# A fused transformer kernel on one core: the hand-kept order of five engines' work, set anew for all 16 groups

## The reference

```python
# layer 0
x = x + tanh(g_xattn[0]) * xattn(layernorm(x), ctx)     # 8 heads, 128 keys, rope, softmax, Wout
h = bitlinear(layernorm(x), w_fc) + gate * low_rank     # 512 -> 2048, ternary weights
x = x + tanh(g_ffn[0]) * bitlinear(relu(h) ** 2, w_proj)
# layer 1
x = x + tanh(g_xattn[1]) * (layernorm(x) @ W1.T + mean(ctx) @ W2.T + b)
h = act_quant(rmsnorm(layernorm(x))) @ ternary(w1).T + b1   # 512 -> 2048
x = x + tanh(g_ffn[1]) * (act_quant(rmsnorm(gelu(h))) @ ternary(w2).T + b2)
```

## Time and profile before

| what | value |
|---|---|
| median of 3 runs | 1218.28 us (1217.88 to 1218.72) |
| the profiled execution's own time | 1217.09 us |
| its span in the trace | 1215.3 us |
| PE busy in the span | 1099.9 us (91%) |
| DVE, ACT, POOL busy | 959.9, 795.2, 590.3 us |
| mean granted clock of PE | 0.977 of full speed |

### The profile page before, as it was taken

One profiled execution on the slowest core, in us unless ns is written; L12 is line 12 of the kernel. 1 busy time (PEld: TensorE's weight loads), 2 busy tenths in 40 slices (PEclk: granted clock), 3 DMA queues, 4 the chain that ended last, 5 costly groups with the idle time before them and its releaser, 6 DMA issues.

```text
span 1215.3 us, 22111 instructions
## 1 busy us (share of the span) xinstructions
PE 1099.9 (91%) x8254; PEld 681.4 (56%) x8542; DVE 959.9 (79%) x1993; ACT 795.2 (65%) x1557; POOL 590.3 (49%) x569
## 2 busy tenths in 40 slices
PE   5766888999999998999999989999999999999995
PEld 5544646565656555564657565654756566564642
DVE  4696689887889797888978897888869677877766
ACT  3887847666675848485756749484675929494624
POOL 2442556454546455464645465554546364563440
PEclk9878999999999999999999999999999999999997
DMA  9959472433427362435434452624345261433132
GB/s 322 361 157 280 148 195 47 95 82 81 105 48 140 57 133 55 104 80 100 88 66 105 66 128 51 126 60 102 71 79 122 48 139 34 102 70 78 23 61 65
DMA packets 281225, 129.93 MB, mean 107 GB/s; under 512 B 254992, under 2 KB 255504, under 8 KB 279440
## 3 DMA queue, kind: packets, MB, share of 16 engines
q1 hardware_dynamic: 280560, 127.57, 45.6%
q10 hardware_dynamic: 560, 0.96, 0.3%
HBM read 57.19 MB, written 8.39 MB: 54 GB/s over the span
## 4 chain that ended last, share of the span: by engine, by line
PE 42%; ACT 23%; DVE 22%; DMA 6%; issue 4%; POOL 3%; SPq 0%; ACTq 0%; DVEq 0%
PE ps L1780 12%; ACT e L949 5%; PE ps L1731 5%; PE ps L1814 4%; PE ps L1682 4%; PE ps L1830 4%; ACT rl L981 4%; PE ps L1764 4%; ACT hid L986 3%; ACT sq L992 2%; DVE st L1342 2%; DVE amax L1075 2%; PE ps L1797 2%; ACT p L957 1%; DMA pt<-p 1%
## 5 line engine op out<-in xcount | busy, mean ns | idle before, releaser
L1764 PE MATMUL ps<-xT,fcT 128*128 128x256 f16 x2048 | 258.7, 274 | 10.0 <-ACT rl L981 9.9
L738 POOL TENSOR_TENSOR rs<-ve,nhalf 128x1 f32<-128x1 f32 x160 | 103.8, 651 | 327.5 <-DVE ve L1347 231.0
L1780 PE MATMUL ps<-pjT,hid 128*128 128x512 fp8e4 x1024 | 232.7, 379 | 5.0 <-issue 2.7
L1764 PEld LDWEIGHTS ps<-xT,fcT 128*128 128x128 fp8e4 x2048 | 199.4, 98 | 49.0 <-ACT rl L981 13.7
L763 POOL TENSOR_TENSOR hid<-sq,hid 128x512 f16<-128x512 f32 x128 | 156.5, 1226 | 104.0 <-ACT sq L992 103.3
L1780 PEld LDWEIGHTS ps<-pjT,hid 128*128 128x128 f16 x1024 | 97.7, 98 | 98.1
L1814 PE MATMUL ps<-w1T,q4T 128*128 128x512 fp8e4 x480 | 118.5, 380 | 9.1 <-DVE h L1491 5.0
L981 ACT ACTIVATE rl<-ps,rsf 128x256 f32<-128x256 f32 x256 | 106.4, 468 | 29.7 <-PE ps L1768 29.5
L949 ACT ACTIVATE e<-ps,nmb,sig 128x128 f32<-128x128 f32 x256 | 113.1, 459 | 16.8 <-DVE nmb L1385 16.7
L1830 PE MATMUL ps<-w2T,hT 128*128 128x512 fp8e4 x480 | 108.4, 379 | 7.3 <-DMA hT<-q 7.3
L1491 DVE SCALAR_TENSOR_TENSOR h<-ps,dqs,b1bc 128x512 f32<-128x512 f32 x120 | 87.9, 743 | 25.8 <-PE ps L1814 24.8
(11 more groups left out here) (234 smaller groups left out, 2032.8 us busy)
## 6 DMA issues: line engine op xcount, KB each, us to landing
...
h<-in_wkvT SPq DMA_DIRECT2D x2, 1024.0 KB, 12.8
hid<-in_w_fc SPq DMA_DIRECT2D x2, 1024.0 KB, 10.9
```

Source lines behind the costliest of these rows:

```text
L738: pool.tensor_tensor(rs[:, n, t:t + 1], ve[:, n, t:t + 1], nhalf[:, :], ALU.pow).then_inc(done, 1)
L1764: pe.matmul(dst, fcT[:, k, f * P:(f + 1) * P], xT2[:, xs, k, :], start=(xs == 0 and k == 0), stop=False)
L1780: mm = pe.matmul(ps[:, FFN0 + t, :], hid[:, xs, c, t * P:(t + 1) * P], pjT[:, c, :], start=(c == 0 and xs == 0), stop=(c == FC - 1 and xs ...
```

## The change

All place numbers of `ORDER` and `PREP` are set anew; nothing else is touched. Each engine holds the same pieces as before. Only a few lines of the table are shown here, since its numbers say little by themselves:

```diff
         ORDER = dict(
             PE=dict(
-                up=((32, 33, 34, 36, 37, 38, 39, 40), (59, 60, 61, 62, 63, 65, 70, 72),
+                up=((33, 34, 35, 36, 37, 38, 39, 40), (59, 60, 61, 62, 63, 65, 69, 70),
...
-                s=((13,), (35,), (58,), (94,), (132,), (167,), (201,), (237,), (273,), (312,), (344,), (384,),
+                s=((13,), (32,), (57,), (96,), (133,), (168,), (200,), (237,), (273,), (308,), (349,), (382,),
```

More of the change, by code:

```diff
@@ new lines, in build @@
+                x1_hi=((0, 2), (8, 31), (48, 75), (107, 112), (135, 146), (165, 174), (200, 202), (231, 235),
+                       (257, 266), (286, 296), (323, 328), (354, 359), (382, 393), (411, 419), (454, 455),
+                       (481, 482)),
+                rot=((17, 18), (51, 52), (85, 86), (116, 118), (151, 152), (178, 181), (209, 210), (240, 242),
+                     (270, 273), (301, 302), (333, 337), (363, 365), (396, 398), (425, 427), (460, 462),
+                     (486, 487)),
@@ L542, in build @@
-            ACT=dict(wq=(3,), k_hi=(17,), v_hi=(20, 22), tanh=(0,), wo=(15,), evac=(6, 13, 16, 23, 28, 36, 37, 38),
-                     rows=(4, 7, 11, 19), whole=(5, 8, 14, 21), low=(32,), wx=(42,),
-                     sums=(27, 33, 40, 43, 44, 45, 46, 47), lift=(52, 55, 58, 74, 75, 79, 81, 85)),
-            POOL=dict(whole=(14, 19, 20, 21), rot_k=(4, 5), csb=(6,), low_zero=(13,)),
-            SP=dict(u=(1,), rows=(6,), ctx=(0,), wk=(3,), wq=(2,), wv=(7,),
-                    piece=(4, 8, 14, 20, 19, 16, 22, 24, 25, 27, 31, 34, 35, 26, 30, 38, 39, 40, 45, 46, 48, 53, 54, 58),
-                    wo=(15,), wc=(11,), wx=(5,), b1=(18,)))
+            PE=dict(k=(2, 3), v=(5, 6), low=(0,), mix=(15,), tern=(4, 7, 12, 14, 16, 19, 20, 21), low_t=(17,),
+                    row_scale=(24,), mean=(30,), spread=(1, 8, 9, 18, 23)),
@@ new lines, in build @@
+            ACT=dict(wq=(4,), k_hi=(15,), v_hi=(14, 20), tanh=(1,), wo=(12,), evac=(6, 10, 16, 22, 27, 36, 37, 38),
+                     rows=(3, 7, 11, 19), whole=(5, 9, 13, 21), low=(32,), wx=(42,),
+                     sums=(26, 33, 40, 43, 44, 45, 49, 50), lift=(54, 59, 66, 72, 74, 77, 79, 80)),
+            POOL=dict(whole=(13, 19, 20, 21), rot_k=(5, 6), csb=(4,), low_zero=(12,)),
+            SP=dict(u=(0,), rows=(13,), ctx=(3,), wk=(4,), wq=(1,), wv=(7,),
+                    piece=(2, 10, 14, 20, 19, 18, 21, 23, 24, 26, 31, 34, 35, 25, 30, 38, 39, 43, 45, 47, 49, 52, 53, 57),
+                    wo=(6,), wc=(5,), wx=(11,), b1=(17,)))
```

249 lines of the change are left out of this document (121 added, 128 removed), and 126 rows, old and new, of tables (down, exp, h, hid).

## The result

| | before | changed |
|---|---|---|
| median | 1218.08 us (1217.59 to 1218.72, 4 runs) | 1207.78 us (1205.83 to 1209.11, 4 runs) |
| ratio to before | | 0.9914, interval 0.9896 to 0.9931 |
| the profiled execution's own time, its span | 1217.09, 1215.3 us | 1205.83, 1204.0 us |

In what follows "waits of PE" are the idle times in the brackets of PE's timeline rows, added up from `low` of group 0 (its own wait not counted) to the last `w2` 0: 70.0 us before, 66.8 after.

The account below looks back on a forecast made before the run. The prediction took PE, busy 1099.9 of 1215.3 us, to bound the kernel, so only its waits could change. Its terms summed to -0.1 us, 1217.0 against the profiled execution's 1217.09, hence a median of 1218.2; range 1208 to 1228.

Parts of the forecast that it names:

- The quantity: Whole kernel: judge an order by cover, the PE work between a piece and the one needing it, against the engines between.
- The start, -1.5: Up to the first values product: scores start some 2 us earlier, the later chain gives part back; -1.5 us.
- Group 0 with group 1, +0.1: 120 to 187 us: waits at scores, `q` and `wx` go, but ACT's later last `up` costs +5.4; together +0.1 us.
- `low` and `up` 0: Groups 1, 10, 13: `up` 0 directly behind `low` waits 1.46 each for the low-rank part; old waits partly go; +2.4 us.
- `w2` 0 of group 2: Cover behind `w1` 3 falls from 19.2 to 14.6 us; PE waits between nothing and 3.1; +1.6 us taken.
- `q`: `q` behind `wo`: more cover in groups 5, 10, 13 gives -2.3, less in group 9 costs +1.0; sum -1.3 us.
- `wx` 1 of group 14: Cover behind `down` 7 falls from 12.8 to 7.4 us; wait 1.6 to 3.5; +2.6 us taken.
- `wx` behind the output write: Three places gain cover, 4.0 us of waits go; group 9 loses its cover, costing 1.2; sum -2.8 us.
- `w2` behind `w1`: `w2` 1 behind `w1` 7: waits in groups 9 and 6 go, group 8 gets +2.0; sum -1.2 us.
- The faster one: Rival for the whole kernel: relu waits, 8.1 us, go and the two middle-group losses stay away; -8.4, 1210 us; chance 0.33.
- The slower rival: `up` rows wait for ACT, with a gap of over 4 us in group 0; +8.8, 1225 to 1227 us; chance 0.31.
- The second price: Group 0's `up` row: after a long gap PE's clock drops to half, adding up to 2.7 us; within the slower rival.

Follow-up runs that it names:

- n2_order: Against the kernel before: all five engines in a new order that counts SP's queue times, with spare in every cover; 1196.58 us, ratio 0.9805.
- n1_order: Against the kernel before: all five engines in a third order, set by covers and DVE's holds by POOL; ratio 1.0189, slower by 23 us.
- x3_pe: The kernel before with PE's order alone made anew; ratio 1.0003 to before, +0.4 us.
- e2_rest: The kernel before up to group 2's scores, the changed kernel's order from there, on all engines; ratio 0.9931 to before, -8.4 us.
- e3_tail: The kernel before up to group 15's scores, the changed kernel's order from there, on all engines; ratio 0.9983 to before, -2.1 us.
- e6_mid: The kernel before with the changed kernel's order only from group 2's to group 15's scores; ratio 0.9982 to before, -2.2 us.
- e1_start: The kernel before with the changed kernel's order only up to `low` of group 0, on all engines; ratio 0.9973 to before, -3.3 us.
- d1_dve: The changed kernel with two 32-column pad writes per layer-norm statistic on DVE instead of one of 1 column; ratio 0.9943 to before.
- n4_both: The changed kernel's order up to `low` of group 0, then that of n3_order, on every engine; ratio 0.9789 to before.
- n5_both: Like n4_both, but the order behind `low` of group 0 set anew for the earlier start; ratio 0.9774 to before.
- e5_relu: The kernel before with six `up` on ACT moved ahead of the exponentials or gelu they stood behind; ratio 1.0059, slower by 7.2 us.
- n3_order: Against the kernel before: all five engines ordered by the rules of n2_order from another start; 1192.73 us, ratio 0.9783.

## Why the prediction was wrong, step by step

*The quantity.* PE's work is the same in all 18 kernels, and its waits go with their times: 49.5 to 52.4 us of waits with medians of 1192 to 1197 us, 62 to 73 with 1208 to 1220, 75.5 with 1226 and 85 with 1243. Inside the second band they don't rank the kernels. Nor are the waits the whole price: PE's busy time for the same matmuls was 1092.9 us in n2_order and 1109.9 in n1_order, at mean granted clocks of 0.976 and 0.962. What failed is that the waits can be read from covers on PE. The mean covers that I compared speak of PE's order alone, and in x3_pe another order of PE alone moved nothing.

*The start, -1.5.* The step that failed is that `low`'s own wait of 5.12 us was left out of the sum. It fell to 1.35. Not even that is its whole size: `mean` came 4.0 us earlier in the changed profile, but in e2_rest, e3_tail and e6_mid, with the start of before, it came at 111.7 to 112.0 us too, and `low` then waited 7.2 to 7.4; in the four other kernels with the new start (e1_start, d1_dve, n4_both, n5_both) it waited 1.3 to 3.0. So the new start is worth 5 us or so there. The scores of group 0 came 4.4 us earlier than in the profile of before, 2.5 earlier than in e6_mid's, where some 2 were expected. But the larger lead was worth little in the end: 3.3 us alone (e1_start), nothing measurable in n4_both.

*Group 0 with group 1, +0.1.* The 0.9 for the scores of group 1 went as forecast. On ACT the size was about right and the place was not: relu and `down` together cost PE 6.3 us more (4.4 to 10.7) where 5.4 stood in the sum, but as a wait of 7.45 in the middle of the `up` row, not as lateness at its end. Wrong were the waits said to go, -4.0: `q` of group 2 waits 3.12 for DVE and `wx` 0 1.49, together 4.6 instead of the two waits' 4.0 of before. From `low` of group 0 to group 2's scores, these included, PE's waits rose by 4.8 instead of 0.1.

*From group 2's scores on, +1.3 for six terms and 0 for the tail.* `low` and `up` 0: +2.5 at L1768, forecast 2.4. `w2` 0 of group 2: 1.89, forecast 1.6. `q`: -0.9, forecast -1.3. These were good. `wx` 1 of group 14: 1.21, forecast 2.6. `wx` behind the output write: -1.4, forecast -2.8. `w2` behind `w1`: all waits for hT fell by 2.8 (with the 1.9 of group 2 in them), so about -4.6 for the rest against -1.2. The step that failed beside this last one is that two lists were put at nothing, without a reason: relu waits at L1764, 8.1 to 1.0, and `w1`'s for L1491, 5.0 to 2.0, while others that were not in the sum (scores, probabilities, `w1` for its transposes) rose by some 4. In all, these waits went from 59.9 to 51.5 us, -8.4 instead of +1.3: -3.4 up to group 15's scores, -5.0 from there. The term for the tail itself, behind the last `down` of group 15, held: 13.8 to 14.6. What went lies just ahead of it, 1.6 at `low` of group 15, 1.1 at its scores, 1.3 for hT and 1.0, 0.8, 0.6 and 0.6 at `w1` and `up`, and no term stood for it. The forecast's own sign of being wrong, idle time that moves by more than 7 us there, came; that of the start, more than 5, did not.

*The rivals.* The faster one named relu and 1210, and the time was 1207.8. Its condition was met in part: relu's waits fell by 7.2, but the two losses that it left out came, at 1.9 and 1.2. That relu's waits are what was won isn't shown: thinning them from ACT's side made the kernel slower (e5_relu). That they fell because DVE and ACT as a whole were set anew is likely, not shown. The slower rival's gap in group 0 came in full, 7.45, and was outweighed. The second price came too, the one that the prediction took from the Trainium skill (page "TensorE: Matmul & The Clock Gate", section "HAM oscillation"): the clock was 0.50 for 3.8 us behind that gap, which cost 1.8 us at `up` 4, within the 2.7 named. The mean clock from 120 to 187 us hides it, 0.96 before and 0.95 after, because before ran from 120.5 to 125 us at 0.50 itself, behind `low`'s wait of 5.12.

*Luck.* The time fell 0.2 us outside the range. The sum missed by more: up to `low` of group 0 by 6.2 us and from group 2's scores on by 9.7, both toward faster, and the block between, 4.7 slower than forecast, took some of it back. That the time ended so near the range is owed to that.

*What stays open.* Which engine's new order makes the waits behind group 2's scores fall; whether middle and tail really give more together (8.4) than apart (4.3); and why n2_order and n3_order, new on all five engines, win more than twice what the changed kernel does. The parts were measured, the mechanism was not.
